# Query preparation of a Perceiver block: the sum of squares as two rounded products, its parts made by GpSimd

## The reference, cut to what matters

```python
x = x + cross(_layernorm(x), ctx_1024)      # then self attention, then the gated layer
q = (hidden_states @ Wq).reshape(B, Sq, H, D)
k = (encoder_hidden_states @ Wk).reshape(B, Skv, H, D)
q = rmsnorm(q, gq)                          # q * rsqrt(mean(q*q) + eps) * gq
k = rmsnorm(k, gk)
scores = einsum('bqhd,bkhd->bhqk', q, k) / sqrt(D)
```

## Time and profile before

| | us |
|---|---|
| median of 3 runs | 1530.04 (1528.72 to 1530.05) |
| the profiled execution, device time | 1526.53 |
| its span | 1524.8 |
| `queries`, up to VectorE's last instruction | 136.2 |
| of it, up to the first matmul of the items | 22.9 |
| barrier and start of `cross_attention` | 136.2 to 139.1 |

### The profile page before, as it was taken

One profiled execution on the slowest core, in us unless ns is written; L12 is line 12 of the kernel. 1 busy time (PEld: TensorE's weight loads), 2 busy tenths in 40 slices (PEclk: granted clock), 3 DMA queues, 4 the chain that ended last, 5 costly groups with the idle time before them and its releaser, 6 DMA issues. The chain is left out here.

```text
span 1524.8 us, 29153 instructions
## 1 busy us (share of the span) xinstructions
PE 1438.0 (94%) x6176; PEld 973.3 (64%) x6176; DVE 1300.6 (85%) x2093; ACT 1156.1 (76%) x4810; POOL 942.6 (62%) x1474
## 2 busy tenths in 40 slices
PE   5996999999999999999999999999999999976886
PEld 3664666666666666666666666666666666853554
DVE  6876888998988898889888998988998988765985
ACT  5886888787888887788878787887878877534763
POOL 4001778887878887788878787878887876010000
PEclk9998999999999999999999999999999999996998
DMA  3000000000000000000000000000001011000000
GB/s 139 37 1 1 1 1 23 7 17 17 8 22 2 23 1 22 2 22 1 22 2 22 10 13 21 3 22 2 23 1 47 1 49 42 1 1 0 8 7 15
DMA packets 9818, 25.05 MB, mean 16 GB/s; under 512 B 736, under 2 KB 6016, under 8 KB 9520
## 3 DMA queue, kind: packets, MB, share of 16 engines
q1 hardware_dynamic: 9648, 23.49, 4.3%
HBM read 22.44 MB, written 1.05 MB: 15 GB/s over the span
## 5 line engine op out<-in xcount | busy, mean ns | idle before, releaser
L807 PE MATMUL psK<-wkh,c_cTh 128*124 128x512 f32 x832 | 509.2, 612 | 6.1 <-DVE c_prod L1235 2.8
L1235 DVE TENSOR_TENSOR c_prod<-psK,c_c 124x512 f32<-124x512 f32 x624 | 427.0, 684 | 65.6 <-PE psK L807 61.7
L1529 POOL TENSOR_TENSOR c_acc<-c_acc,c_prob 123x1024 f32<-123x1024 f32 (+1 forms) x192 | 459.1, 2391 | 2.6 <-issue 1.4
L827 PE MATMUL psO<-c_prob,raw 123*128 123x512 f32 (+1 forms) x832 | 424.9, 591 | 0.0
L1021 ACT ACTIVATE c_unused<-c_prod 124x128 f32<-124x128 f32 x832 | 247.5, 299 | 110.5 <-DVE c_prod L1235 110.5
L1252 DVE TENSOR_TENSOR c_prob<-psS,c_ss 124x512 f32<-124x512 f32 x416 | 286.9, 690 | 50.2 <-PE psS L818 34.8
L807 PE MATMUL psK<-wkl,c_cTh 128*124 128x512 f32 x832 | 328.6, 395 | 0.0
L1027 ACT ACTIVATE c_prob<-c_prob,shift 124x1024 f32<-124x1024 f32 x208 | 238.9, 1149 | 56.7 <-DVE c_prob L1252 45.4
L1242 DVE TENSOR_REDUCE c_ss<-c_prod 124x8 f32<-124x1024 f32 x208 | 253.8, 1220 | 7.2
L1013 ACT ACTIVATE c_unused<-psK 124x128 f32<-124x128 f32 x832 | 218.8, 277 | 52.9 <-PE psK L807 37.4
L807 PEld LDWEIGHTS psK<-wkh,c_cTh 128*124 128x124 f32 x832 | 154.4, 186 | 143.6 <-issue 88.7
(11 more groups left out here) (312 smaller groups left out, 2311.5 us busy)
## 6 DMA issues: line engine op xcount, KB each, us to landing
raw<-in_ctx SPq DMA_DIRECT2D x16, 799.5 KB
raw<-in_L_xattn_Wq SPq DMA_DIRECT2D x3, 512.0 KB, 9.7
xs<-in_x SPq DMA_DIRECT2D x1, 1024.0 KB, 5.7
big<-in_L_xattn_Wk SPq DMA_DIRECT2D x1, 1024.0 KB, 9.0
c_prod<-in_L_xattn_Wo SPq DMA_DIRECT2D x1, 1024.0 KB, 5.2
out<-s_y SPq DMA_DIRECT2D x8, 128.0 KB, 1.7
big<-in_L_ffn_W_qkv SPq DMA_DIRECT2D x1, 768.0 KB, 12.9
c_wqkv<-in_L_attn_W_qkv SPq DMA_DIRECT2D x1, 768.0 KB, 15.9
```

What stands on the lines that cost most here:

```text
L807: last = nc.tensor.matmul(psK[0:ROWS, c % 2, :], x[:, slot, :], w[:, cols], start=(n == 0), stop=(n == len(terms) - 1))
L827: nc.tensor.matmul(psO[:, half, :], raw[0:rows, b, tile, :], prob[0:rows, probs(v), half * BANK:(half + 1) * BANK], start=(tile == 0), sto ...
L1235: nc.vector.tensor_tensor(prod[:, k % 2, c - GRAM, :].rearrange("p (h c) -> p h c", c=CD), psK[0:ROWS, c % 2, :].rearrange("p (h c) -> p h ...
L1529: nc.gpsimd.tensor_tensor(acc[0:rows, batch % 2, :], acc[0:rows, batch % 2, :], prob[0:rows, probs(s), :], ALU.add).then_inc(S.acc, 1)
```

## The change

1. The squares are split on GpSimd: `squareh` = square + 0, rounded to float32r (an addition with the one-column tile `blank`, broadcast), and `squarel` = square - squareh, which is written over the square. TensorE sums them with two float32r matmuls, `onesr` by squareh and by squarel, into psS. This is done for item o = n - 2 in place of m = n - 1.
2. ScalarE's logarithm is of item o and stands first in a step instead of last; the square waits for `squarel` of two items before.
3. VectorE's first Newton product is written back into psS instead of the SBUF tile `scaled`; the low part `qgl` stands ahead of it. TensorE's psS bank is now free after `root`, not after `newton`.
4. The low parts of Wq: GpSimd makes blocks 0 and 1, with `wkl` between them; VectorE makes blocks 2 and 3, ahead of the items. The last block of Wq lies in a free part of `T.queries`, and each block is loaded by two DMAs.
5. `raw` is zeroed in four parts, each after the squares of an item on GpSimd (items 20 to 23), and the first context load starts after the last of them. The gain's steps are n = 25 and 28 instead of 28 and 30.

```diff
         def _(sp):
             for q, sem in enumerate(wq_there):
-                sp.dma_start(wq(q), dram["L0_xattn_Wq"].rearrange("(k p) n -> p k n", p=P)[:, :, quad(q)]).then_inc(sem, 16)
+                for k in range(WC):
+                    sp.dma_start(wq(q)[:, k, :, :], halved(dram["L0_xattn_Wq"].rearrange("(k p) n -> p k n", p=P)[:, :, quad(q)])[:, k, :, :]).then_inc(sem, 16)
...
-            for q in range(KC):
-                pool.wait_ge(S.wqh, q + 1)
-                nc.gpsimd.tensor_tensor(wql[:, :, quad(q)], wq(q), wqh[:, :, quad(q)].bitcast(F32), ALU.subtract).then_inc(S.wql, 1)
...
-            nc.gpsimd.memset(T.raw[:, :], 0.0).then_inc(S.zeroed, 1)
...
+            def step(n, m, o):
+                if m is None:
+                    return
+                pool.wait_ge(S.square, m + 1)
+                if m >= 2:
+                    pool.wait_ge(S.total, m - 1)
+                nc.gpsimd.tensor_tensor(squareh[:, m % 2, :], square[:, m % 2, :], blank[:, :].broadcast_to([P, BANK]), ALU.add).then_inc(S.squareh, 1)
+                pool.wait_ge(S.squareh, m + 1)
+                nc.gpsimd.tensor_tensor(squarel[:, m % 2, :], square[:, m % 2, :], squareh[:, m % 2, :].bitcast(F32), ALU.subtract).then_inc(S.squarel, 1)
+                if m in ZERO_AT:
...
+                    nc.gpsimd.memset(T.raw[:, ZERO[ZERO_AT.index(m)]], 0.0).then_inc(S.zeroed, 1)
...
-                if m is not None:
-                    pe.wait_ge(S.square, m + 1)
-                    if m >= 2:
-                        pe.wait_ge(S.newton, m - 1)
-                    nc.tensor.matmul(psS[:, m % 2, :], T.ones[:, :], square[:, m % 2, :], start=True, stop=True).then_inc(S.total, 1)
                 if o is not None:
+                    if o == 0:
+                        pe.wait_ge(S.onesr, 1)
+                    pe.wait_ge(S.squarel, o + 1)
+                    if o >= 2:
+                        pe.wait_ge(S.root, o - 1)
+                    nc.tensor.matmul(psS[:, o % 2, :], onesr[:, :], squareh[:, o % 2, :], start=True, stop=False)
+                    nc.tensor.matmul(psS[:, o % 2, :], onesr[:, :], squarel[:, o % 2, :], start=False, stop=True).then_inc(S.total, 1)
...
+            for q in range(2, KC):
+                dve.wait_ge(S.wqh, q + 1)
+                nc.vector.tensor_tensor(halved(wql[:, :, quad(q)]), wq(q), halved(wqh[:, :, quad(q)]).bitcast(F32), ALU.subtract).then_inc(S.wql, 1)
...
-                    nc.vector.scalar_tensor_tensor(scaled[:, :], psS[:, o % 2, :], float(D * EPS), half[:, :], ALU.add, ALU.mult).then_inc(S.newton, 1)
...
+                    nc.vector.scalar_tensor_tensor(psS[:, o % 2, :], psS[:, o % 2, :], float(D * EPS), half[:, :], ALU.add, ALU.mult).then_inc(S.newton, 1)
                     dve.wait_ge(S.newton, o + 1)
-                    nc.vector.scalar_tensor_tensor(root[:, :], scaled[:, :], 1.5, y[:, o % 2, :], ALU.subtract, ALU.mult).then_inc(S.root, 1)
+                    nc.vector.scalar_tensor_tensor(root[:, :], psS[:, o % 2, :], 1.5, y[:, o % 2, :], ALU.subtract, ALU.mult).then_inc(S.root, 1)
```

More of the change, by code:

```diff
@@ L188 @@
 PREP_SEMS = ("x gains wk wq0 wq1 wq2 wq3 consts gprod made stats moments centred lnT lnTh lnTl wkT wkTh wkTl wqh wql "
-             "wkh wkl gram gramh graml zeroed context m8 m2 sel causal iota selb wgate wqkv turn turned gT gtop gall")
+             "wql0 onesr blank wkh wkl gram gramh graml zeroed context m8 m2 sel causal iota selb wgate wqkv turn turned gT gtop gall")
 Q_SLOTS = 3
 X_SLOTS = 2 * BANK // DIM
-ITEM_SEMS = "q square qgh qgl total log y half newton root qw out"
+ITEM_SEMS = "q square squareh squarel qgh qgl total log y half newton root qw out"
 def queries(nc, T, psum, dram):
@@ L212, in queries @@
         xTh, xTl = sb("xTh", [P, WC, NPAIR * P], F32R), sb("xTl", [P, WC, NPAIR * P], F32R)
-        square, log, half = sb("square", [P, 2, BANK]), sb("log", [P, BANK]), sb("half", [P, BANK])
-        y, scaled, root = sb("y", [P, 2, BANK]), sb("scaled", [P, BANK]), sb("root", [P, BANK])
+        with ExitStack() as shared:
+            square = shared.enter_context(nc.sbuf_tensor("q_square", [P, 2, BANK], F32))
+        squarel = sb("squarel", [P, 2, BANK], F32R)
+        squareh, onesr, blank = sb("squareh", [P, 2, BANK], F32R), sb("onesr", [P, P], F32R), sb("blank", [P, 1])
+        log, half = sb("log", [P, BANK]), sb("half", [P, BANK])
+        y, root = sb("y", [P, 2, BANK]), sb("root", [P, BANK])
         qgh, qgl = sb("qgh", [P, Q_SLOTS, BANK], F32R), sb("qgl", [P, Q_SLOTS, BANK], F32R)
@@ L251, in queries @@
         gain_row, gain_all = psM[0:1, 0:P], psM[:, P:P + 1]
-        GAIN_AT, GAIN_ALL_AT = 28, 30
+        GAIN_AT, GAIN_ALL_AT = 25, 28
+        ZERO_AT = (20, 21, 22, 23)
+        ZERO = [slice(2 * NT * CD * n // 4, 2 * NT * CD * (n + 1) // 4) for n in range(4)]
         def out(n):
@@ L455, in _ @@
             act.wait_ge(S.made, 1)
+            nc.scalar.activation(onesr[:, :], T.ones[:, :], ACT.Copy).then_inc(S.onesr, 1)
             def step(n, m, o):
+                if o is not None:
+                    act.wait_ge(S.total, o + 1)
+                    nc.scalar.activation(log[:, :], psS[:, o % 2, :], ACT.Ln, scale=1.0 / D, bias=T.eps[:, :]).then_inc(S.log, 1)
                 if n is not None:
@@ L476, in step @@
                     nc.scalar.activation(half[:, :], y[:, o % 2, :], ACT.Square, scale=float(np.sqrt(0.5 / D))).then_inc(S.half, 1)
-                if m is not None:
-                    act.wait_ge(S.total, m + 1)
-                    nc.scalar.activation(log[:, :], psS[:, m % 2, :], ACT.Ln, scale=1.0 / D, bias=T.eps[:, :]).then_inc(S.log, 1)
                 if n is not None:
```

43 lines of the change are left out of this document (30 added, 13 removed).

## The result

The changed kernel took **1519.64 us** (median of 6 runs, 1516.58 to 1522.08); the kernel before, beside it on the same chip, 1528.58 (6 runs, 1527.35 to 1530.05). The ratio is 0.9939, interval 0.9922 to 0.9957: 9 us faster. The forecast was 1524.0, range 1520.0 to 1528.2. The medians themselves differ by 8.9, 5.1 and 7.4 us, 7.1 on average, so the size of the gain is known to about 1 us.

What follows compares the result with a forecast made beforehand. A ring over three engines bound `queries` at 3.14 us an item, VectorE's 2.70 next. Last `out` 32.5 + 29 x 2.75 + 8.3 + 8.7 = 129.3, 6.0 earlier: 1530.0 - 6.0 = 1524.0 us, range 1520.0 to 1528.2.

Steps and rivals of the forecast that it cites:

- the ring over the sums' bank: Old `queries` items: waits through TensorE, ScalarE and VectorE take 6.28 us for two items, 3.14 each, setting the pace.
- the floor: Changed `queries` items: VectorE's four instructions, 0.65, 0.72, 0.72 and 0.61, sum to 2.70 us an item.
- rival 2: VectorE's root reading PSUM costs 0.065 us more an item, 1.9 in all, giving 1525.9 us; chance 0.12.
- rival 3: GpSimd and VectorE hold each other in the items: pair 3.6 us, 24.7 more, 1548.7 us; chance 0.05.
- The front's chain: Start of `queries`: low-part blocks and first squares queue on VectorE and GpSimd; first `out` at 36.9, 3.8 us lost.
- The load: First context load, after the last memset: lands at 126.0, 4 us before the barrier at about 130.2, so hidden.
- 29 plain steps: Steps of `queries` without extra work: 2.75 us an item, bounds 2.70 and 2.90.
- Gram steps: Three `queries` steps with Gram work: 1.6 us extra each, 4.8 in all, bounds 3.9 to 5.4.
- transposed weights and gain: Extra work in single `queries` steps: four transposed weights at 0.75 us each, 3.0 (bounds 2.0 to 3.6), plus gain 0.5.
- end, from the last full step: Last two `queries` steps, without `qgl` or new square: last `out` starts 8.7 us after step 31's logarithm.
- The 0.05: Supplement per item on VectorE's 2.70 us, because four rings lie within 0.1 us of it; pace taken as 2.75.
- Rival 4: More gain: front without holding (1.7), pace 2.70 (1.5), extras at lower bounds (2): 5.2 more, 1518.8 us; chance 0.08.

Runs made afterwards that it cites:

- f32_sum: Changed kernel with one float32 product of ones by `squareh` in place of the float32r pair, `squarel` left out of the sum: 1525.74 us, ratio 0.9983.

## Why the forecast was off

**What held.** TensorE was at its limit and the ring over the sums' bank set 3.15: `f32_sum` shows the first, and leaves 4.8 us for the second. The float32r pair takes 0.47. VectorE's four instructions are the floor, and the order and start distances (0.65, 0.72, 0.72, 0.61) are theirs to 0.01. PSUM as source costs nothing that can be seen: the product that writes it and the root that reads it take 0.69 each, so rival 2 falls. The two fixed costs in the Trainium skill (VectorE: DVE Perf Modes, the TRN2 errata) would by an estimate set them 0.06 us apart from the SBUF case; no row shows that. GpSimd is hidden with idle time before its pairs, and rival 3 falls. The front's chain is the one laid out: block 2, `wkl`, block 3, block 1, the first pair, each held as expected. It ran 0.5 to 0.9 us early throughout, and Wk was there 0.54 earlier than in the profile of before; at an equal landing the front loses 3.6 us where 3.8 were forecast. The load lands at 125.4 (forecast 126.0).

**What was mis-sized**, on the way to the last `out`, forecast 129.3 and measured 128.43:

| term | forecast | measured | difference |
|---|---|---|---|
| first `out` | 36.9 | 36.19 | -0.7 |
| 29 plain steps | 79.75 (2.75 each) | 78.6 (2.71) | -1.2 |
| Gram steps | 4.8 | 5.7 | +0.9 |
| transposed weights and gain | 3.5 | 2.0 | -1.5 |
| end, from the last full step | 4.3 | 4.6 | +0.3 |
| low clock behind the first item | 0 | 1.4 | +1.4 |

The 0.05 that I added to VectorE's floor for rings that lie close to it was not there: the pace is the floor to 0.01. The transposed weights cost 0.3 to 0.5 each (3.0 to 3.2 an item against 2.71) where I took 0.75, the sum of ScalarE's and TensorE's parts; with the gain that is less than the lower bounds given. The Gram step costs 1.9, more than the upper bound: 1.3 us of waiting for the work of TensorE and ScalarE, and 0.6 for VectorE's own `gram_low` (L579), which had room in the old pace and which I put at nothing, though VectorE was the new floor. The rows are:

```profile
55.77 0.68 DVE L579 TENSOR_TENSOR wkl<-psM,wkh 128x512 fp32r<-128x512 f32 x1
56.37 0.74 DVE L591 SCALAR_TENSOR_TENSOR q_qgl<-psK,gcol,q_qgh 128x512 fp32r<-128x512 f32 x1
```

And the low clock in 32 to 35 us, which three of six profiles have, wasn't in the sum at all. Rival 4 came true in part: the pace at its lower bound and the transposed weights below theirs, but not a front without holding. These errors leave 0.9 us by which the last `out` was forecast too late.

**The step that failed** is the last one of the sum, from the stage to the time: "Span 1524.8 - 6.0", and then the same 6.0 taken from a median of 1530.0, as if base and later stages were exact. The mechanism held; what was mis-sized are the base, the scatter and, by less, the stage's 6.0. The result lies 4.4 us under the forecast:

- 1.5 us are the base. 1530.04 is the median of three runs; those three and three more have 1528.58, and the other comparisons 1528.14, 1528.36, 1529.22 and 1529.12.
- 0.8 us are the stage, which gave 6.8 us in the first profile, and 6.9 on average over six (5.0 to 8.2, by where Wk lands and where the low clock falls).
- The remaining 2.1 us belong to no term of the sum. The later stages, put at nothing, were 2.3 us shorter in the first profile and 2.0 and 2.2 longer in the two others of the same program, so I take this for scatter.

The lower bound, 1520.0, held none of the three. That the time fell just outside it is bad luck in part: the same kernel had medians of 1523.05 and 1521.73 in the other comparisons, both inside the range. And that "the rest of the program keeps its instructions" costs nothing came true (the loop takes 925.1 us before and 924.9 after), but without a reason that I had looked at: nine more instructions on VectorE made that loop 12 to 15 us longer.

## What to carry to other kernels

When a ring over several engines is opened, take the sum of the start distances of the next engine as the new pace, and cost the steps with extra work by what they add on that engine, not by their price in the old pace. (In this one case no supplement was needed, though four rings lay within 0.1 us.) Give the low end of a range the scatter of the base, of the front and of the stages that don't change, not only the terms' bounds. Before a small shift is put down to an edit, take away what a transfer's landing gave: here the first `out` followed Wk one for one. If a small edit in a straight stretch changes a later loop, look for "issue" rows on one engine in the loop before explaining it by time.

## What was not expected of the hardware

- Nine VectorE instructions more ahead of the loop made it 12 to 15 us longer (939.9 and 937.7 against 925.2 us), five 3 us; a chain of 6.50 us and one of 1.71 did nearly the same.
- GpSimd's addition of a broadcast column takes 1.04 us for 512 columns, neither half of the 1.89 for 1024 nor the 1.29 of two full inputs.
- A VectorE instruction with two SBUF inputs beside GpSimd's additions costs 0.11 us at the median, where the earlier trace rows showed 1.2. Why it is so little the runs don't show.
- The granted clock falls in a stage that is busy otherwise: 0.72 from 32 to 38 us, in three of six profiles of one and the same stage, which cost 1.2 to 1.4 us each time. TensorE's idle time before it was 1.9 to 2.4 us in all six.
